# A four-stage convolution network on one core: column tiles of the middle convolutions, statistics by sums, and the order of the first pair

## The reference

```python
x = x + L0(gn(x))   # q, k, v: 3x3 convs; bias: a 7x7 conv; attention over rows with a softmax over channels; times v
x = x + L1(gn(x))   # input and weights quantised to -127..127 (one scale for the whole tensor), 3x3 conv 32->32
x = x + L2(gn(x))   # mean over pixels -> 32x32 layer -> relu -> a 3x3 kernel for every sample and channel (depthwise)
x = x + L3(gn(x))   # 3x3 local std, its min and max over all samples; two fixed 21x21 filters; relu(center - std * surround)
```

## Time and profile before

| | us |
|---|---|
| median of 3 runs (1253.83 to 1255.99) | 1254.89 |
| the profiled execution | 1254.0 |
| its span | 1252.2 |

### The profile page before, as it was taken

The page is one execution under the profiler, slowest core; times in us unless marked ns, Lnnn a source line. Parts: engine busy times, 40 slices in busy tenths (PEclk is TensorE's granted clock), DMA queues, the critical chain, the costliest instruction groups (busy, mean ns, idle before and its releaser), DMA issues.

```text
span 1252.2 us, 37089 instructions
## 1 busy us (share of the span) xinstructions
PE 1101.1 (88%) x16332; PEld 800.7 (64%) x16332; DVE 840.9 (67%) x1033; ACT 544.7 (44%) x667; POOL 386.6 (31%) x380
## 2 busy tenths in 40 slices
PE   2789999999999999999524668877889999999997
PEld 2789999999999999999422334332334444444443
DVE  6444486685748568473687899989988664566444
ACT  3243635646373555524239846637771121122110
POOL 1534656546455663645300033413220000000000
PEclk9989999999999999999867678899999999999999
DMA  5010020200102010100002232322344644656550
GB/s 204 3 41 35 3 73 3 73 3 19 57 3 73 3 39 3 40 3 4 2 7 69 70 87 70 87 65 68 77 131 105 205 132 152 184 155 183 157 140 34
DMA packets 52621, 89.69 MB, mean 72 GB/s; under 512 B 9307, under 2 KB 37211, under 8 KB 51452
## 3 DMA queue, kind: packets, MB, share of 16 engines
q1 hardware_dynamic: 44776, 80.56, 22.5%
q10 hardware_dynamic: 7700, 6.89, 1.9%
HBM read 36.89 MB, written 11.99 MB: 39 GB/s over the span
## 4 chain that ended last, share of the span: by engine, by line
PE 69%; DVE 21%; ACT 4%; issue 3%; DMA 1%; SPq 1%; DVEq 0%; ACTq 0%
PE psum L1465 37%; PE psum L1697 15%; PE psum L1711 9%; PE psum L1500 2%; DVE small L873 2%; DVE arena L971 1%; DVE small L696 1%; PE psum L1598 1%; DVE arena L889 1%; DVE arena L978 1%; ACT arena L1226 1%; ACT arena L1232 1%; DVE arena L990 1%; DVE small L580 1%; PE psum L1490 1%
## 5 line engine op out<-in xcount | busy, mean ns | idle before, releaser
L1465 PE MATMUL psum<-arena 128*128 128x64 f16 (+2 forms) x11904 | 511.9, 207 | 16.0 <-DMA arena<-arena 12.6
L1465 PEld LDWEIGHTS psum<-arena 128*128 128x128 f16 x11904 | 495.1, 98 | 31.6 <-issue 12.8
L619 DVE TENSOR_TENSOR arena<-psum,arena 128x512 f32<-128x512 f32 x128 | 87.9, 692 | 191.6 <-PE psum L1465 164.4
L1697 PE MATMUL psum<-arena 128*128 128x512 f16 (+2 forms) x936 | 192.3, 366 | 0.0
L1697 PEld LDWEIGHTS psum<-arena 128*128 128x128 f16 x936 | 92.2, 99 | 98.7 <-issue 3.5
L1366 POOL TENSOR_TENSOR arena<-arena 128x256 f16<-128x256 f32 x63 | 50.6, 804 | 292.2 <-ACT arena L1140 292.2
L1370 POOL TENSOR_SCALAR arena<-arena,constants_f 128x256 f16<-128x256 f16 x126 | 136.7, 1112 | 0.0
L1136 ACT ACTIVATE arena<-arena 128x256 f16<-128x256 f32 x63 | 26.5, 421 | 221.6 <-issue 121.5
L1711 PE MATMUL psum<-arena 120*128 120x512 f16 (+1 forms) x528 | 116.8, 379 | 0.0
L1711 PEld LDWEIGHTS psum<-arena 120*128 120x128 f16 (+1 forms) x528 | 51.4, 97 | 61.9 <-issue 0.2
L1598 PE MATMUL psum<-arena 128*64 128x512 f16 x576 | 74.4, 421 | 13.2 <-DMA arena<-arena 13.1
(11 more groups left out here) (197 smaller groups left out, 1515.5 us busy)
## 6 DMA issues: line engine op xcount, KB each, us to landing
arena<-in_filter_tables SPq DMA_DIRECT2D x8, 1280.0 KB, 8.6
X<-in_x SPq DMA_DIRECT2D x16, 512.0 KB, 4.6
arena<-arena SPq DMA_DIRECT2D x32, 256.0 KB, 4.0
out<-X SPq DMA_DIRECT2D x16, 512.0 KB, 4.0
arena<-edge_columns SPq DMA_DIRECT2D x90, 80.0 KB
arena<-arena SPq DMA_DIRECT2D x48, 132.0 KB, 2.4
arena<-edge_columns ACTq DMA_DIRECT2D x70, 80.0 KB
arena<-arena SPq DMA_DIRECT2D x32, 140.0 KB, 2.5
```

The costliest lines, as they stand in the source:

```text
L619: v.tensor_tensor(out_, bank_rows(k), biasrow, ALU.add).then_inc([g.staged0, g.staged1][k], 1)
L1465: last = mm(conv[k][:, c0:c1], win[:, kk, lx, y + e, dx:dx + W, :].rearrange("p w s -> p (w s)"), wt[:, lw, d, w0:w1], start=(n == 0), sto ...
L1697: mm(bank[4 * s + 2 * f + hf][:, C * lo:C * hi], tb[:, f, d + 2, lt], xt[s][:, hf, lx, YP + d + lo:YP + d + hi].rearrange("p y c -> p (y c)"),
```

## The change

1. `conv1` and `conv2` use two copies of the rows, `a12` unshifted on all partitions and `b12` with partitions 64 to 127 shifted by one e. Row classes 1 and 2 are made from `a12`, class 0 and class 3 from `b12`. A product has 32 columns and writes 32 PSUM partitions; four stand where two of 64 columns stood. The shift is two DMAs of 64 partitions.
2. ACT's cast and DVE's low part each take all 128 partitions; POOL's low part goes.
3. The statistics of x2 are `bn_stats` for even samples only. For odd ones, and for all of x3, DVE's addition gives the sum of X (`accum_out`) and ACT's `squares` the sum of squares. `kernels_of` starts one turn later, at the head of the turn; the third statistics are spread over three turns.
4. In the first pair the two parts of pair 1's normalisation, its low part and the weight maximum are moved forward among the evacuations, on DVE, ACT and PE.

The diff, cut to its core, eight spaces of indent taken off:

```diff
     def shift(k, parts):
-        for p0, p1, src, dst in ((0, 32, 0, 0), (32, 96, 0, 1), (96, 128, 1, 1)):
+        for p0, p1, dst in ((0, 64, 0), (64, 128, 1)):
             sp.dma_start(b12[p0:p1, k, 0:parts, dst:dst + NY, :].rearrange("p l e w -> p l (e w)"),
-                         a12[p0:p1, k, 0:parts, src:src + NY, :].rearrange("p l e w -> p l (e w)")
+                         a12[p0:p1, k, 0:parts, 0:NY, :].rearrange("p l e w -> p l (e w)")
                          ).then_inc(b_in[k], 16)
...
-    evacuate_rows(0, 0, 3)
+    evacuate_rows(0, 0, 1)
     norm0_a(1)
+    evacuate_rows(0, 1, 2)
+    norm0_b(1)
+    evacuate_rows(0, 2, 3)
+    v.tensor_reduce(one[0], raw1, AX.X, ALU.max, apply_absolute_value=True).then_inc(g.w1_max, 1)
     evacuate_rows(0, 3, 4)
-    norm0_b(1)
+    low_a(1, 1)
+    evacuate_rows(0, 4, 5)
     quantise_weights()
-    evacuate_rows(0, 4, 6)
-    low_a(1, 1)
+    evacuate_rows(0, 5, 6)
     norm0_a(2)
     evacuate_rows(0, 6, 8)
...
     def add1(n):
         xb = X[:, n].rearrange("p y w -> p (y w)")
         v.wait_ge(g.c1_done, n + 1)
-        v.scalar_tensor_tensor(xb, slot_psum(n), one[4], xb, ALU.mult, ALU.add).then_inc(g.x2_sum, 1)
+        v.scalar_tensor_tensor(xb, slot_psum(n), one[4], xb, ALU.mult, ALU.add,
+                               accum_out=sums2[:, 2 * n:2 * n + 1] if n % 2 else None).then_inc(g.x2_sum, 1)
     def low2(n):
-        v.wait_ge(g.ah2, 2 * n + 1)
-        w_ = a12[0:96, n % NS, :, 0:NY, PAD1:PAD1 + W]
-        v.tensor_tensor(w_[:, 1], y12[0:96, n % NS], w_[:, 0], ALU.subtract).then_inc(g.al2, 1)
+        v.wait_ge(g.ah2, n + 1)
+        w_ = a12[:, n % NS, :, 0:NY, PAD1:PAD1 + W]
+        v.tensor_tensor(w_[:, 1], y12[:, n % NS], w_[:, 0], ALU.subtract).then_inc(g.al2, 1)
...
     def add2(n):
         v.wait_ge(g.c2_done, n + 1)
         xb = X[:, n].rearrange("p y w -> p (y w)")
-        v.scalar_tensor_tensor(xb, slot_psum(B + n), 1.0 / (XS * KS), xb, ALU.mult, ALU.add
-                               ).then_inc(g.x3_sum, 1)
+        v.scalar_tensor_tensor(xb, slot_psum(B + n), 1.0 / (XS * KS), xb, ALU.mult, ALU.add,
+                               accum_out=sums2[:, 2 * n:2 * n + 1]).then_inc(g.x3_sum, 1)
     def kernels_of(h, step):
         of, half = slice(NT * h, NT * h + NT), slice(2 * NT * h, 2 * NT * h + 2 * NT)
         if step == 0:
-            v.wait_ge(g.x2_ready, NT * (h + 1))
+            v.wait_ge(g.x2_ready, NT // 2 * (h + 1))
+            v.wait_ge(g.x2_sq, NT // 2 * (h + 1))
+            v.tensor_scalar(by_two[0], by_two[1], 1.0 / PIX, None, ALU.mult)
...
+    late = slice(NT + 1, B)
+
+    def sums_of_x3(ready, of):
+
+        v.wait_ge(g.x3_sum, ready)
+        v.wait_ge(g.x3_sq, ready)
+        v.tensor_scalar(mvx[:, 2 * of.start:2 * of.stop], sums2[:, 2 * of.start:2 * of.stop], 1.0 / PIX, None,
+                        ALU.mult).then_inc(g.gst_mv, 1)
+
+    early = slice(0, NT + 1)
     for turn in range(LEAD + B + LAG):
         n1, n2 = turn - LAG1, turn - LEAD
+        for h in range(2):
+            if 0 <= n1 - NT * (h + 1) - 1 < 5:
+                kernels_of(h, n1 - NT * (h + 1) - 1)
         if turn < B:
             round1(turn)
         if 0 <= n1 < B:
         if 0 <= n2 < B:
             spread_kernels(n2)
             low2(n2)
-        if 0 <= n1 < B:
-            sample_stats(n1, g.x2_sum, g.x2_ready, bn)
+        if 0 <= n1 < B and n1 % 2 == 0:
+            sample_stats(n1)
         if n2 >= LAG:
             add2(n2 - LAG)
-            sample_stats(n2 - LAG, g.x3_sum, g.x3_ready, bn0)
-        for h in range(2):
-            if 0 <= n1 - NT * (h + 1) < 5:
-                kernels_of(h, n1 - NT * (h + 1))
-        if n2 - LAG == NT:
-            v.wait_ge(g.x3_ready, NT + 1)
-            all_stats(3, tp[0])
+        if n2 - LAG == NT + 2:
+            sums_of_x3(NT + 1, early)
+        if n2 - LAG == NT + 3:
+            take_sums(3, tp[0])
+            root_a(3)
+        if n2 - LAG == NT + 4:
+            root_b(3)
             link(v.tensor_scalar(scale3, rs, XS, None, ALU.mult))
             set_scale(scale3, shift3, g.l3_scale)
...
-    highs(0, 0, 4)
+    highs(0, 0, 2)
     norm0_root(1)
     norm0(1, 1)
-    highs(0, 4, 8)
+    highs(0, 2, 8)
...
     def quantised(n):
         a.wait_ge(g.rounded, n + 1)
         wait_reuse(a, g.c1_done, n - NS + 1)
-        for p0, p1, e in ((0, 96, 0), (96, P, 1)):
-            a.activation(a12[p0:p1, n % NS, 0, e:e + NY, PAD1:PAD1 + W], y12[p0:p1, n % NS], ACT.Identity,
-                         bias=unround[p0:p1]).then_inc(g.q1_ready, 1)
+        a.activation(a12[:, n % NS, 0, 0:NY, PAD1:PAD1 + W], y12[:, n % NS], ACT.Identity, bias=unround
+                     ).then_inc(g.q1_ready, 1)
+
+    def squares(n, summed, done, before):
+        a.wait_ge(summed, n + 1)
+        wait_reuse(a, done, before)
+        a.activation(squares12, X[:, n].rearrange("p y w -> p (y w)"), ACT.Square,
+                     accum_out=sums2[:, 2 * n + 1:2 * n + 2]).then_inc(done, 1)
     def high2(n):
         k = n % NS
         a.wait_ge(g.l2_scale, n // NT + 1)
         wait_reuse(a, g.al2, n - NS + 1)
-        wait_reuse(a, g.al2_pool, n - NS + 1)
         a.activation(y12[:, k], X[:, n], ACT.Identity, **scaled(n)).then_inc(g.y2, 1)
         a.wait_ge(g.y2, n + 1)
         a.wait_ge(g.c1_done, B - NS + n + 1 if n < NS else B)
         wait_reuse(a, g.c2_done, n - NS + 1)
-        for p0, p1, e in ((0, 96, 0), (96, P, 1)):
-            a.activation(a12[p0:p1, k, 0, e:e + NY, PAD1:PAD1 + W], y12[p0:p1, k], ACT.Copy).then_inc(g.ah2, 1)
+        a.activation(a12[:, k, 0, 0:NY, PAD1:PAD1 + W], y12[:, k], ACT.Copy).then_inc(g.ah2, 1)
     a.wait_ge(g.zero12, 1)
-    for turn in range(LEAD + B - 1):
+    for turn in range(LEAD + B + LAG):
         n2 = turn - LEAD + 1
         if turn < B:
             normalise1(turn)
         if 1 <= turn <= B:
             quantised(turn - 1)
         for h in range(2):
-            if turn - LAG1 - NT * (h + 1) == 1:
+            if turn - LAG1 - NT * (h + 1) == 2:
                 all_stats(h + 1)
-        if n2 == NT + 5:
+        if n2 == NT + LAG + 4:
             all_stats(3)
-        if n2 >= 0:
+        if 0 <= n2 < B:
             high2(n2)
+        n1, n3 = turn - LAG1 - 1, n2 - LAG - 2
+        if 0 <= n1 < B and n1 % 2:
+            squares(n1, g.x2_sum, g.x2_sq, n1 // 2)
+        if 0 <= n3:
+            squares(n3, g.x3_sum, g.x3_sq, n3)
...
+        if n == 0:
+            squares(B - 1, g.x3_sum, g.x3_sq, B - 1)
...
     for n in range(B):
-        k = n % NS
-        gp.wait_ge(g.ah2, 2 * (n + 1))
-        w_ = a12[96:P, k, :, 1:1 + NY, PAD1:PAD1 + W]
-        gp.tensor_tensor(w_[:, 1], y12[96:P, k], w_[:, 0], ALU.subtract).then_inc(g.al2_pool, 1)
-
-    gp.wait_ge(g.al2_pool, B)
...
-    conv0(0, 0, 0, 3)
+    conv0(0, 0, 0, 2)
+    stat0(1)
+    conv0(0, 0, 2, 3)
     windows_ready(0)
     conv0(0, 0, 3, 4)
-    stat0(1)
     pe.wait_ge(g.w1_max, 1)
     spread(one[0], g.w1_spread)
     conv0(0, 0, 4, 8)
...
+    w1v = w1q[:, :].rearrange("p (o d c) -> p o d c", o=G, d=3)
     b_in = [g.b_0, g.b_1, g.b_2, g.b_3]
+
+    source_of = ((b12, 0), (a12, 0), (a12, 0), (b12, 1))
     def conv1(n):
         k = n % NS
-        pe.wait_ge(g.q1_ready, 2 * (n + 1))
-        pe.wait_ge(b_in[k], 48 * (n // NS + 1))
+        pe.wait_ge(g.q1_ready, n + 1)
+        pe.wait_ge(b_in[k], 32 * (n // NS + 1))
         wait_reuse(pe, g.x2_sum, n - NPS + 1)
         for hf in range(2):
             for dx in range(3):
-                for win, src in enumerate((a12, b12)):
-                    e = 8 * hf + win
-                    last = mm(slot_banks(n)[hf][64 * win:64 * win + 64, :], w1v[:, win, dx],
-                              src[:, k, 0, e:e + 8, dx:dx + W], start=(dx == 0), stop=(dx == 2),
-                              skip_group_check=True)
+                for row, (src, e) in enumerate(source_of):
+                    last = mm(slot_banks(n)[hf][C * row:C * row + C, :], w1v[:, row, dx],
+                              src[:, k, 0, 8 * hf + e:8 * hf + e + 8, dx:dx + W], start=(dx == 0),
+                              stop=(dx == 2), skip_group_check=True)
         last.then_inc(g.c1_done, 1)
     def conv2(n):
         k = n % NS
-        pe.wait_ge(b_in[k], 48 * (n // NS + 1 + B // NS))
-        pe.wait_ge(g.ah2, 2 * (n + 1))
+        pe.wait_ge(b_in[k], 32 * (n // NS + 1 + B // NS))
+        pe.wait_ge(g.ah2, n + 1)
         pe.wait_ge(g.al2, n + 1)
-        pe.wait_ge(g.al2_pool, n + 1)
         pe.wait_ge(g.k2_ready, n + 1)
         pe.wait_ge(g.x2_sum, min(B, B + n - NPS + 1))
         wait_reuse(pe, g.x3_sum, n - NPS + 1)
-        kw = k2[:, k].rearrange("p l (w d m) -> p l w d m", w=2, d=3)
+        kw = k2[:, k].rearrange("p l (o d c) -> p l o d c", o=G, d=3)
         for hf in range(2):
             for dx in range(3):
                 for lx, lw in ((0, 0), (0, 1), (1, 0)):
-                    for win, src in enumerate((a12, b12)):
```

(20 more changed lines are left out.)

48 lines of the change are left out of this document (22 added, 26 removed).

## The result

The changed kernel takes **1201.79 us** (median of 4 runs, 1198.46 to 1203.64) where the kernel before takes 1255.44 (4 runs, 1253.83 to 1256.1): a ratio of 0.957, 95% interval 0.955 to 0.960. Forecast were 1205, in a range from 1197 to 1224, with a chance of 0.88 for faster. The profiled execution took 1201.51 us, its span is 1199.7, 52.5 less than the 1252.2 of before.

What follows compares the result with a forecast made beforehand. The prediction took PE, with waits behind DVE, to bound the first pair, ACT conv1 and DVE conv2. From 1254.0 it took 13.1 (first pair), 14.3 (conv1) and 23 (conv2), adding 1 (L3): 1205 us, range 1197 to 1224.

Steps and rivals of the forecast that it cites:

- First pair, -13.1: First pair: without PE's two waits and the low clock behind them, pair 1 starts at 88.2 instead of 101.3, 13.1 us less.
- tightest point: First pair: half-row 4's evacuation ends at 48.1, half-row 6 needs it at 48.5; 0.4 us of slack.
- catch up: First pair: `highs` and `lows` of rows 2 and 3, behind the normalisation, finish during half-rows 8 and 9, within 7.8 us.
- rival D: First pair keeps a wait at half-row 6 and the clock falls: 6 us stay, 1211; chance 0.22 shared with Rival C.
- conv1, -14.3: conv1 turns: shorter ACT and DVE work lets conv2 begin at 715.4 instead of 729.70, 14.3 us less.
- conv2, -23: conv2: PE becomes the longest at 4.2 us a sample; the stage takes 75.7 us instead of 98.6, 23 less.
- L3, +1: Start of L3: `prepare3` now follows the last squares and DVE's group step waits for it, 1 us more.
- Rival A: conv2: only two column tiles stream at a time, 7.9 us a sample, 1264 in total, slower; chance 0.11.
- Rival B: conv2: the four tiles' weight loads are not fully hidden, 5.6 us a sample, 22 more, 1227; chance 0.12.
- rule on weight loads within a row group: conv2 tiles: a weight load runs beside products in flight only when the row group differs, which speaks against the tiles.
- estimate of 5.1 us: conv2: from the skill's 2.38x for three column tiles, a sample would take some 5.1 us and the sum be 1220.
- Rival C: conv2 stays limited by hand-overs at kernel steps, 10 us idle where 1.5 was left, 1213; chance 0.22 shared with rival D.

Runs made afterwards that it cites:

- e6: Changed kernel with the first pair reordered again: row 2's high parts ahead of ACT's normalisation, row 4 evacuated ahead of the low part; 1196.77 us.
- e4: Changed kernel with conv2's products reordered: per half of the rows, 18 products of tiles 0 and 1, then 18 of tiles 2 and 3; 1215.26 us.
- e7: Changed kernel without conv2's products of the input's low part (48 a sample in place of 72); 1192.15 us.
- e8: Kernel before without conv2's products of the input's low part (24 a sample in place of 36); 1254.62 us, ratio 1.001.
- e3: Kernel before with only the statistics changed to sums on DVE and ACT; two tiles, three copies and POOL's part stay; 1231.33 us.
- e10: Kernel of e6 with conv2's shifted copy in two steps, the high part issued as soon as ACT has cast it; 1195.34 us.
- e2: Kernel before with only two row copies, four column tiles, whole casts and low parts, no POOL; statistics stay `bn_stats` on DVE; 1234.6 us.

## Why the prediction was right, step by step

The total of 1205 against 1201.8 is closer than its terms, and that part is luck: the first pair gave 3.8 us less than forecast and conv1 4.8 more. The mechanisms of the two middle stages held; of the signs named, conv2's length (74.6 in 74 to 78), PE's share there (94%), its sample (3.96 to 4.11) and DVE's low part (1.22) came out, while the start of conv2 (55.1 us after the first `normalise1`, not 58 to 61) and the first pair did not.

- *First pair, -13.1.* It gave 9.3. The tightest point that I named held: half-row 4's evacuation ended at 47.9, and half-row 6 did not wait. The failed step is that `highs` and `lows` of rows 2 and 3 "catch up": POOL's first two steps of row 2 took 6.0 us beside DVE's low part instead of 1.8, and PE waited 2.62 us, with a stretch at lower clock behind it (0.50 from 68 to 70 us). e6 takes the wait away and reaches 88.8. This is rival D's kind at another half-row: 3.8 us of the 13.1 stayed, where D had 6.
- *conv1, -14.3.* It gave 19.1. The turns are not where it was mis-sized: they are shorter than forecast (2.17 us at first and 5.39 for two with a square, not 2.32 and 5.7), but ACT then idles 2.4 us for DVE at the kernels' steps, and the first `high2` begins 42.8 us after the first `normalise1`, 42.6 forecast. Mis-sized are what follows: conv1 of sample 13 ended at 42.9 where I had walked it to 46.1, `generated` took 2.84 us at full clock where I had the 5.28 of the trace of before, and the 1 us allowed for reading the sums showed nowhere. The other way, the first copy took 4.9 us from DVE's low part to the first product, where I had 3.3.
- *conv2, -23.* It gave 24.0: 74.6 us against 75.7. PE's sample is 3.96 in a stream (4.2 forecast), and 4.11 alone. The waits are 3.25 us after the first sample where I had 1.5; they are all for copies. The first samples run at the lower of the clock's two levels (0.50, 1.2 GHz), as forecast.
- *L3, +1.* 0.3.
- *Rival A* (two tiles at a time, 7.9 us a sample) did not come about. e4 adds that its price was wrong too: even an order made for it takes 4.84, because PE starts products of other tiles ahead. *Rival B*: a group of four costs 0.22 us, its loads nothing. PEld is busy 33.8 us of conv2 beside PE's 70.0, and does not stand on the chain there. So the Trainium skill's rule on weight loads within a row group ("TensorE: Matmul & The Clock Gate", Part 3, what overlaps) is not borne out here for four tiles either, nor is the estimate of 5.1 us from its table. *Rival C*: PE waited 3.25 us for copies, before samples 5, 8 and 15, as its sign said, but a third of the 10 us that it named.
- *The bound.* That PE holds conv2 after the change and did not before is shown by e7 and e8, that DVE did before by its busy share (92.9 of 98.6 us) and by e3. What my expectations got wrong is how the parts share the gain: in e3 the statistics alone bring 22.0 of conv2's 24.0, and the tiles alone 12.1; their own merit is in conv1, where they halve ACT's casts, and most of that comes only together with the statistics (19.1 us against 7.5 and 2.0).

## What to carry to other kernels

Price a part of a change stage by stage against the engine that will be the floor there, since parts whose total gains happen to add may overlap in one stage and need each other in another. When an instruction is moved beside another engine's, look in the trace for rows where the two already ran side by side, and take that duration, not the typical one. To learn who sets the pace, leave work out of the suspect in both kernels: the same edit was worth 8 to 10 us after the change and nothing before.

## What the runs showed of the hardware

- Column tiles queue apart: with the products of two tiles issued in blocks of 18 or 36, the other two tiles' products start ahead of their turn, by some 7 as worked out from the times (4.84 and 6.54 us for 72 products, 3.96 when all four alternate, 7.9 by 36 pairs one after another).
- POOL's f32 subtractions run 3 to 4.4 times as long beside DVE's 96x2048 one (2.52 to 2.98 us against 0.67 for 128x256, 3.49 against 1.16 for 128x512).
- A 264 KB copy within SBUF lands in 2.6 to 2.8 us over partitions 32 to 96 with copies of 132 KB around it, and in 3.9 over 0 to 64 or 64 to 128 with another of 264 KB; each DMA more costs SP's queue 0.63 to 0.72 us on the chain.
- Reading an accumulator is an instruction of its own, 186 ns on ACT and 82 on DVE.
- The clock fell to 0.61 in one execution (e10) behind 24 small f32 products without a wait of PE, and stayed at 1.00 in another (e6) of nearly the same kernel, on another chip.
- The same 24 products took 5.28 us at a clock of 0.50 in the trace of before and 2.84 at 1.00 in those of e2, e3 and the changed kernel.
